# Attention groups on one core: tiled matmuls gathered into one batch a step, row maxima taken in pairs, two scores behind one wait, the loop over groups written out

## What is computed

```
h = b + sum of 4 table rows per token          # token ids of the last four positions
h = h + attention(layernorm(h))                # 32 query heads, 8 key/value heads, head size 32, causal, RoPE
h = h + ffn(layernorm(h))                      # x @ W_base.T + b, plus a low-rank update through a Fourier matrix
```

```
scores = q @ k.T / sqrt(32); scores above the diagonal = -1e20
attn   = softmax(scores)          # exp(score - row maximum) / sum
out    = attn @ v
```

## Time and profile before

| What | us |
|---|---|
| median of three runs | 4028.03 |
| profiled execution, its own time | 4027.74 |
| its span, first to last instruction | 4025.9 |
| part_b's loop: group 1 | 147.5 |
| groups 2 to 14 together | 1965.6 |
| group 15 | 135.6 |

### The profile page before, as it was taken

One profiled execution on the slowest core, in us unless ns is written; L12 is line 12 of the kernel. 1 busy time (PEld: TensorE's weight loads), 2 busy tenths in 40 slices (PEclk: granted clock), 3 DMA queues, 4 the chain that ended last, 5 costly groups with the idle time before them and its releaser, 6 DMA issues. The chain is left out here.

```text
span 4025.9 us, 69672 instructions
## 1 busy us (share of the span) xinstructions
PE 3776.8 (94%) x22272; PEld 2433.5 (60%) x22272; DVE 2292.9 (57%) x3912; ACT 1626.7 (40%) x3068; POOL 1589.7 (39%) x525
## 2 busy tenths in 40 slices
PE   2889888899999999999999999999999779999999
PEld 2777777655555555555555555555555248888887
DVE  3666656676566566566566566566566144443443
ACT  2222222155555555555555555555555521010110
POOL 5222330045544544544544544545544513232322
PEclk9999999799999999999999999999999979999999
DMA  8877785411111111111111111111110243334432
GB/s 242 209 182 193 202 200 133 97 44 47 33 46 47 33 46 47 33 46 47 33 46 47 33 46 47 33 46 47 33 46 25 70 138 94 93 87 94 90 96 65
DMA packets 240124, 325.95 MB, mean 81 GB/s; under 512 B 62795, under 2 KB 139595, under 8 KB 239859
## 3 DMA queue, kind: packets, MB, share of 16 engines
q1 hardware_dynamic: 221426, 255.22, 23.7%
q0 software_dynamic: 18432, 67.12, 7.6%
HBM read 223.67 MB, written 97.52 MB: 80 GB/s over the span
## 5 line engine op out<-in xcount | busy, mean ns | idle before, releaser
L714 DVE TENSOR_REDUCE mpart<-mx_ps 128x1 f32<-128x512 f32 (+3 forms) x2560 | 1455.1, 606 | 841.4 <-PE mx_ps L769 455.3
L672 ACT ACTIVATE probs<-st_ps 128x512 f32<-128x512 f32 (+3 forms) x2560 | 1297.7, 533 | 1093.6 <-PE st_ps L798 535.7
L656 POOL TENSOR_TENSOR sums<-probs 128x2048 f32<-128x2048 f32 (+1 forms) x320 | 1182.6, 3696 | 1256.8 <-PE den_ps L827 1171.3
L795 PE MATMUL st_ps<-qs,k_score 98*128 98x512 f32 (+3 forms) x2560 | 1087.2, 428 | 31.2 <-issue 25.3
L766 PE MATMUL mx_ps<-k_max,qs 96*128 96x512 f32 (+3 forms) x2560 | 985.4, 393 | 14.5 <-POOL consts_r L647 14.1
L795 PEld LDWEIGHTS st_ps<-qs,k_score 98*128 98x128 f32 x2560 | 482.1, 189 | 814.5 <-ACT probs L672 659.6
L810 PE MATMUL o_ps<-probs,vs 128*32 128x512 f32 (+3 forms) x5120 | 606.9, 546 | 0.0
L766 PEld LDWEIGHTS mx_ps<-k_max,qs 96*128 96x128 f32 x2560 | 495.1, 195 | 48.2 <-POOL consts_r L647 14.3
L202 POOL DMA_INDIRECT hbuf<-in_tok_table,idx x128 | 194.1, 1517 | 352.3 <-ACT xn L233 231.2
L1030 POOL TENSOR_TENSOR h<-h,bb 128x1024 f32<-128x1024 f32 x32 | 105.1, 3283 | 543.2 <-DVE xn_c L1128 543.2
L386 PE MATMUL qk_ps<-x_hi,w_hi 128*128 128x512 f32 x640 | 259.7, 406 | 51.2 <-ACT rotation L245 31.8
(11 more groups left out here) (103 smaller groups left out, 3819.9 us busy)
## 6 DMA issues: line engine op xcount, KB each, us to landing
qs<-q_hi_scratch SPq DMA_DIRECT2D x128, 256.0 KB, 4.5
h_scratch<-hbuf SPq DMA_DIRECT2D x32, 512.0 KB, 3.5
q_hi_scratch<-rot_hi SPq DMA_DIRECT2D x64, 256.0 KB, 2.6
q_lo_scratch<-rot_lo SPq DMA_DIRECT2D x64, 256.0 KB, 3.3
qs<-q_lo_scratch SPq DMA_DIRECT2D x64, 256.0 KB, 5.5
o_scratch<-o_sb SPq DMA_DIRECT2D x64, 256.0 KB
o_in<-o_scratch SPq DMA_DIRECT2D x32, 512.0 KB, 4.4
o_in<-recip_scratch SPq DMA_DIRECT2D x128, 128.0 KB, 7.9
```

The costliest lines, as they stand in the source:

```text
L656: nc.gpsimd.tensor_tensor(sums[:, p % SUM_SLOTS, :, j * P:CT], a, b, ALU.add).then_inc(sum_done, 1)
L672: nc.scalar.activation(probs[:, s % SLOTS, h, j * P:CT], st_ps[:, u % SCORE_BANKS, 0:CT - j * P], ACT.Exp, scale=float(HD) ** -0.5).then_i ...
L714: nc.vector.tensor_reduce(mpart[:, h * TPC + t, kc:kc + 1], mx_ps[:, n % MAX_BANKS, 0:w], AX, ALU.max).then_inc(max_done, 1)
L795: mm = nc.tensor.matmul(st_ps[:, u % SCORE_BANKS, 0:w], k_score[0:M_ROW + 2, kt * P:(kt + 1) * P], qs[c][0:M_ROW + 2, h, j * P:CT], start= ...
```

## The change

- The group loop is written out: sixteen groups of straight code on every engine, and constants in place of registers. The small semaphore increments that stood between a wait on a register and a DMA go too.
- Tiled matmuls: values now come at the end of the step and lag one step instead of two. The denominators of a pair are cut into two halves of the columns; one half follows the values in each step. A step therefore has one batch of column-tiled matmuls, values and then half a pair's denominators.
- Maxima: 80 pairs of heads instead of 160 single ones. The PSUM is the same four banks, used as two slots of two banks. VectorE reduces both heads with one instruction. A step has two pairs (in some three), one after score 1 and one after score 2. The turn comes after three more pairs (`TURN_AFTER` 3) instead of after five more maxima.
- Scores: head 0 waits for all exponentials of the step before, head 1 waits for nothing, heads 2 and 3 wait for exponentials 0 and 1 of their own step.
- ScalarE copies `o_ps` out at the start of the step after next, ahead of the exponentials, and `den_ps` after the second exponential instead of the first.

```diff
-    return [(c, kc, t, h) for c in range(QC) for kc in range(c + 1) for t in range(TPC) for h in range(GROUP)]
+    return [(c, kc, t, h) for c in range(QC) for kc in range(c + 1) for t in range(TPC) for h in range(0, GROUP, 2)]
...
-SCORE_BANKS, MAX_BANKS = 2, 4
-VALUE_LAG, DEN_LAG = 2, 4
+SCORE_BANKS, MAX_SLOTS = 2, 2
+VALUE_LAG, DEN_LAG = 1, 4
 LEAD, FIRST_LEAD = 20, 14
-TURN_AFTER = 5
+TURN_AFTER = 3
...
         def groups(eng, group):
-            group(0, True, False)
-            with eng.Fori(1, GROUPS - 1) as g:
-                group(g, False, False)
-            group(GROUPS - 1, False, True)
+            for g in range(GROUPS):
+                group(g, g == 0, g == GROUPS - 1)
...
                 for s in range(NS):
+                    k = s - VALUE_LAG - 1
+                    if k % NS in LAST_OF and not (first and k < 0):
+                        take_o(g if k >= 0 else g - 1, step if k >= 0 else step - NS, LAST_OF.index(k % NS))
                     for h in range(GROUP):
                         exps(unit, pair, s, h)
                         k = s - DEN_LAG - 1
-                        if h == 0 and k % NS in LAST_OF and not (first and k < 0):
+                        if h == 1 and k % NS in LAST_OF and not (first and k < 0):
                             take_den(pair if k >= 0 else pair - PAIRS, LAST_OF.index(k % NS))
...
-                nc.vector.tensor_reduce(mpart[:, h * TPC + t, kc:kc + 1], mx_ps[:, n % MAX_BANKS, 0:w], AX, ALU.max
+                nc.vector.tensor_reduce(mpart[:, h:h + 2, t, kc], mx_ps[:, n % MAX_SLOTS, :, 0:w], AX, ALU.max
                                         ).then_inc(max_done, 1)
...
+                for k in range(2):
+                    out = mx_ps[:, n % MAX_SLOTS, k, 0:w]
+                    mm = nc.tensor.matmul(out, qs[c][0:K_ROWS, first_head + k, t * P:(t + 1) * P],
+                                          k_max[0:K_ROWS, kc * CT:kc * CT + w], start=True, stop=not diagonal)
+                    if diagonal:
+                        mm = nc.tensor.matmul(out[:, w - P:w], identr, mqk, start=False, stop=True)
                 mm.then_inc(max_ready, 1)
...
-                if not (is_first(g) and u < SCORE_BANKS):
-                    pe.wait_ge(exp_done, unit + u - (SCORE_BANKS - 1))
+                if h == 0 and not (g == 0 and s == 0):
+                    pe.wait_ge(exp_done, unit + s * GROUP)
+                if h >= SCORE_BANKS:
+                    pe.wait_ge(exp_done, unit + s * GROUP + h - 1)
...
+            def denominators(g, pair, p, part):
...
+                alone = (j * P, (j + 1) * P) if diagonal else (0, 0)
+                half = (j * P + CT) // 2 if diagonal else CT // 2
+                if part == 0:
+                    pe.wait_ge(sum_done, pair + p + 1)
...
+                lo, hi = ((alone[1], half), (half, CT))[part]
+                if lo < hi:
                     for h in range(GROUP):
+                        mm = nc.tensor.matmul(den_ps[h * HD:(h + 1) * HD, lo:hi], ones[:],
+                                              sums[:, p % SUM_SLOTS, h, lo:hi], start=False,
+                                              stop=closing and part == 1)
...
                     for h in range(GROUP):
                         scores(g, unit, s, h)
-                        for more, n in entries[len(entries) * h // GROUP:len(entries) * (h + 1) // GROUP]:
-                            give(g + more, ring + more * NE, n)
-                        if h == GROUP // 2 - 1:
-                            lagging_values(g, unit, s)
+                        if h in (1, 2):
+                            for more, n in entries[len(entries) * (h - 1) // 2:len(entries) * h // 2]:
+                                give(g + more, ring + more * NE, n)
+                    lagging_values(g, s)
                     lagging_denominators(g, pair, s)
```

More of the change, by code:

```diff
@@ L690, in group @@
                         k = s - DEN_LAG - 1
-                        if h == 0 and k % NS in LAST_OF and not (first and k < 0):
+                        if h == 1 and k % NS in LAST_OF and not (first and k < 0):
                             take_den(pair if k >= 0 else pair - PAIRS, LAST_OF.index(k % NS))
-                    k = s - VALUE_LAG
-                    if k % NS in LAST_OF and not (first and k < 0):
-                        take_o(g if k >= 0 else g - 1, step if k >= 0 else step - NS, LAST_OF.index(k % NS))
             groups(act, group)
@@ L764, in row_scores @@
                 w = (t + 1) * P if diagonal else CT
-                out = mx_ps[:, n % MAX_BANKS, 0:w]
-                mm = nc.tensor.matmul(out, qs[c][0:K_ROWS, h, t * P:(t + 1) * P],
-                                      k_max[0:K_ROWS, kc * CT:kc * CT + w], start=True, stop=not diagonal)
-                if diagonal:
-                    mm = nc.tensor.matmul(out[:, w - P:w], identr, mqk, start=False, stop=True)
+                for k in range(2):
[4 more added lines that the diff above has]
+                        mm = nc.tensor.matmul(out[:, w - P:w], identr, mqk, start=False, stop=True)
                 mm.then_inc(max_ready, 1)
@@ L812, in values @@
                 mm.then_inc(pv_done, 1)
-            def denominators(g, pair, p):
+            def denominators(g, pair, p, part):
                 c, kt, j = STEPS[2 * p]
                 diagonal, opening, closing = kt >= c * TPC, 2 * p in FIRST_OF, 2 * p + 1 in LAST_OF
-                pe.wait_ge(sum_done, pair + p + 1)
-                if opening and not (is_first(g) and c == 0):
-                    pe.wait_ge(den_copied, g * QC + c)
-                if diagonal:
-                    for h in range(GROUP):
-                        nc.tensor.matmul(den_ps[h * HD:(h + 1) * HD, j * P:(j + 1) * P], ones[:],
-                                         probs[:, 2 * p % SLOTS, h, j * P:(j + 1) * P], start=opening, stop=False)
-                at = (j + 1) * P if diagonal else 0
-                for h in range(GROUP):
-                    mm = nc.tensor.matmul(den_ps[h * HD:(h + 1) * HD, at:CT], ones[:],
-                                          sums[:, p % SUM_SLOTS, h, at:CT], start=False, stop=closing)
-                mm.then_inc(den_done, 1)
@@ L831, in lagging_values @@
-            def lagging_values(g, unit, s):
+                alone = (j * P, (j + 1) * P) if diagonal else (0, 0)
+                half = (j * P + CT) // 2 if diagonal else CT // 2
+                if part == 0:
+                    pe.wait_ge(sum_done, pair + p + 1)
+                    if opening and not (g == 0 and c == 0):
+                        pe.wait_ge(den_copied, g * QC + c)
+                    if diagonal:
+                        for h in range(GROUP):
+                            nc.tensor.matmul(den_ps[h * HD:(h + 1) * HD, alone[0]:alone[1]], ones[:],
+                                             probs[:, 2 * p % SLOTS, h, alone[0]:alone[1]], start=opening, stop=False)
@@ L832, in lagging_values @@
                 k = s - VALUE_LAG
                 if k >= 0:
[L834 to L836 removed]
+                    values(g, k)
+                elif g > 0:
+                    values(g - 1, k + NS)
             def lagging_denominators(g, pair, s):
                 k = s - DEN_LAG
[L840 to L841 removed]
                 if k >= 0:
[L843 to L845 removed]
+                    denominators(g, pair, k // 2, k % 2)
+                elif not g == 0:
+                    denominators(g - 1, pair - PAIRS, (k + NS) // 2, k % 2)
```

116 lines of the change are left out of this document (45 added, 71 removed).

## The result

The changed kernel takes 3992.51 us (median of four runs, 3987.36 to 3993.11), the kernel before, run beside it, 4028.63 us (4026.15 to 4031.72). The ratio is 0.9907, 95% interval 0.989 to 0.9924: 0.9% faster, where 2.2% were forecast. The time lies 4.5 us above the top of the predicted range. The profiled execution took 3987.36 us, 47.1 us more than the 3940.3 that the sum gave for it.

The account below looks back on a forecast made before the run. TensorE's own stream was taken as the bound (94% busy). Branches -48, 14 groups x 3.1 us = -43.4, and +2 for each end group gave -87.4 from 4027.7: 3940 us, range 3902 to 3988.

Parts of the forecast that it names:

- The loop, -48.1: Groups 2 to 14: without 13 branches each starts as group 1 does, 147.5 us, saving 48.1 us, slow clock included.
- Rival 3: Group loop written out: straight code of sixteen groups stalls for instructions as often as the branch did; 3988 us, chance 0.05.
- The batches, -0.34 per isolated batch: Column-tiled batches on TensorE: two steps have two instead of three, saving 0.34 us per two steps; columns stay the same.
- The exponential's wait, 1.19 and one a full step: Full steps: score 2 waits for exponential 0 until 1.19 us, once in each step; two steps take 7.52 us.
- A slot is wanted again a step later, long after its reduction ... hidden: 0: Paired maxima on VectorE: two reductions make 2.8 us at most in a 3.76 us step, so they cost nothing.
- Group 0, +2: Group 0 catches up its lead in six steps with four pairs and two slots: 5 us more, less 3.1.
- The term for the catching up: Six steps of group 0: TensorE stands until VectorE has emptied the first slot, estimated 0.85 us more in each.
- The start, 0: Stretch up to the first exponential: forecast unchanged at 790.1 us.
- Group 15, +2: Group 15 has no maxima after step 19: eight pairs of full steps cost 3.8 us, its first half saves 1.6.
- Rival 4: Two-bank reductions above 1.88 us let VectorE set the step, since only two slots exist; 4280 us, chance 0.05.
- TensorE waiting for `mx_ps` slots: A sign in the changed kernel's trace that would show the forecast wrong: TensorE stands for the slots of the maxima.
- rivals on batches and loop: Batches bring nothing, 3983 us, chance 0.14; straight code stalls for instructions as the branch did, 3988 us, chance 0.05.

## Why the prediction was wrong

- **The loop, -48.1: right.** Alone it gave 147.4 a group (147.5 forecast) and 47.5 us less of span; by the ratio, 0.9864, it is 55 us with an interval from 47 to 62, so 48.1 is at its lower end. Rival 3 is out. Of the 48 us, 26 stand at the 13 branches themselves: there the next score follows the denominators after 2.69 to 3.38 us instead of 0.99. At most 15 more, half of 30.6, are the clock, which stood at 0.50 for 30.6 us in groups 1 to 14, behind 8 of the 13 branches and not behind the other five. The page "Runtime: NRT & Kernel Launch" of the Trainium skill, section "Instruction fetch mechanics", says that a taken branch breaks the sequential prefetch when its target is not among the instructions at hand. By that rule the loop should cost something at every turn, and the trace agrees: 3.57 us at the branch in the median, none in straight code.
- **The batches, -0.34 per isolated batch: right.** Shown by the reverse: one more per step costs 0.32 to 0.33 on full steps. The page "TensorEngine Tiling (Array Packing)" of the Trainium skill says in its section "Key Properties" that switching the tiling mode needs a drain; that a switch costs something is what this run shows, the drain itself it does not. That a group gained what was forecast is in part luck. Between the kernel with the loop alone and that with single maxima it is 3.4 us (147.4 to 144.0), 3.1 forecast; but in group 5 the eight pairs of diagonal steps are 4.4 shorter, where 2.7 were put, and the twelve of full steps 1.0 longer, where they were to be 0.4 shorter. Part of that is only that values with a lag of one fall into another pair.
- **The exponential's wait, 1.19 and one a full step: right** (1.18 and 3.74 to 3.76). Groups are 144.0 without the pairs, 144.4 forecast. What it did not see is that a split of the maxima other than the one in the diff would take this wait away; that is worth 2.5 to 2.9 us a group. A wait that is met costs nothing, so the 0.34 behind an unmet one belongs to the stall and not to the instruction.
- **"A slot is wanted again a step later, long after its reduction ... hidden: 0": this is the step that failed.** The reduction itself was sized right (1.22 us for two banks, forecast 1.1 to 1.4), and against a whole step it is hidden. But the sum of VectorE's time over a step isn't what TensorE waits for. With two slots the third request of a step waits for the first one's reduction, and some steps have a third request: a turn, which takes a whole slot for 16 rows, or a third pair. In group 5, steps 4 and 39 are 0.98 and 0.87 us longer than with single maxima, and they are the two with a wait for a slot. Steps 25 and 33 are 0.23 and 0.45 longer without any: there the turn comes first and is taken early, but it stands alone behind score 1, covers little of the exponential's time, and both pairs fall behind score 2. That is the coarse split into pairs and not the slots. Step 33 in the timeline of TensorE, after:

```profile
1668.84 0.73 PE L772 MATMUL st_ps<-qs,k_score 98*128 98x512 f32 x2
1669.41 0.27 PE L748 MATMUL mx_ps<-ident_b,mcol 128*16 128x128 f32 x1
1670.03 0.50 PE L772 MATMUL st_ps<-qs,k_score 98*128 98x512 f32 x1 [0.34 <-ACT probs L648]
1670.37 1.09 PE L740 MATMUL mx_ps<-k_max,qs 96*128 96x512 f32 x4
```

In all, pairs cost 2.25 us a group, 31.4 us in groups 1 to 14 (in steps 9 and 29 the single maxima are 0.22 us longer each, with five of them where the pairs have four). The kernel with single maxima takes both causes away at once; that slots alone can do it is shown by the one with two slots of one bank.
- **Group 0, +2: mis-sized.** The forecast was 155.9, measured 170.7, and 13.5 of it are the pairs (157.2 without them). The term for the catching up, 0.85 us in each of six steps, was about right: set beside the kernel with single maxima, by the starts of the scores, these steps (3, 7, 11, 15, 19, 23) are 0.34 to 1.22 us longer, 4.1 together. What was missing is the clock: steps 4 to 6, which run at half clock behind the first of them, are 7.1 us longer. With the catching up gone the stretch at half clock went too, and group 0 took 148.6.
- **The start, 0: wrong by 4.4.** The same cause, at a granted clock of 0.50: from the first maxima to the first exponential it is 37.8 us, and 33.4 both before and with single maxima. The timeline of TensorE, after, around a turn of the start:

```profile
770.18 0.38 PE L748 MATMUL mx_ps<-ident_b,mcol 128*16 128x128 f32 x1
771.59 1.22 PE L740 MATMUL mx_ps<-k_max,qs 96*128 96x512 f32 x2 [1.03 <-DVE mpart L689]
```

- **Group 15, +2: right by mechanism,** 137.0 against 136.3; two full steps of it took 7.07 us, forecast 6.90. That the kernel with only the loop written out also shows 137.1 there is something else, 6.8 us at half clock, which its windows view has:

```profile
3109.70:3116.20 6.50, 6.24 (x30) 1.94 (x29) 0.00 (x0) 2.48 (x6) 4.38 (x1) 0.53 0.00 0
```

- **Rival 4** named the right place, VectorE behind two slots, but let it decide only from 1.88 us a pair. It decides at 1.22 already, in some steps (4 and 39). "TensorE waiting for `mx_ps` slots" stood among the signs of a wrong forecast, and is what the trace shows.
- **The range:** it was cut at 3988 by rivals on batches and loop. A case between "pairs cost nothing" and 4280 was missing.

As a chain in ratios to the kernel before: loop 0.9864, batches and order with single maxima 0.9752, pairs on top 0.9907. The best kernel is 0.9659: written-out loop, one batch a step, single maxima in four slots, all behind score 1.

## What to carry to other kernels

When a buffer is regrouped into fewer, larger slots, count the requests of the worst step and not the mean: a producer in a fixed order stands as soon as it asks for one more slot than there are before the first is emptied, and a small user (here a turn of 16 rows) takes a whole slot. Merging work on an engine that nobody waits for earns nothing and can cost exactly this. And put the matmuls that cover a wait all in the place where the wait is, not evenly between the scores.

## What the runs showed of the hardware

- A taken branch of the hardware loop held TensorE's sequencer for 3.57 us in the median (3.27 to 3.96), while ScalarE's, VectorE's and GpSimd's took 0.04 to 0.06. Behind 8 of the 13 the clock stood at half for 3.4 us (6.8 once). The same code written out had neither at any boundary between groups.
- Half clock came in a busy stretch, but short stalls alone don't explain it. In the kernel with two one-bank slots there were six stretches of 3.4 us at 0.50 in groups 1 to 14; the groups with one take 171.6 us, those with two 173.0 and 173.1, the others 169.9 to 170.1, so one costs 1.6 us. They begin in step 3 (stalls of 0.32 and 0.53 us) or step 32 (0.40), but the same steps have the same stalls in all fourteen groups, and the clock fell behind 6 of these 28. The windows view of one:

```profile
1698.00:1701.30 3.30, 3.30 (x22) 1.82 (x21) 0.86 (x2) 0.36 (x2) 0.78 (x1) 0.50 0.41 87
```

- Moving between full matmuls and column-tiled batches costs 0.32 to 0.34 us per isolated batch in full steps, and the trace shows it as busy time.
- A reduction over two banks with two results takes 1.22 us, one over a single bank 0.68: 0.14 us saved per pair.
